# Moving the quantisation of the feed-forward weights from a stage of its own into the attention and layer-norm stages

## The chip, the cores and the metric

The kernel runs on the 8 cores of one Trainium2 chip. Each core computes one of the 8 sequences of the batch with all the weights; the cores exchange nothing. The metric is the device time in microseconds (us) of the slowest core; the time of a kernel is the median of its runs. The profile shows one execution, on its slowest core (core 1).

## The reference

One layer: attention with rotary embedding and a residual layer norm, then a feed-forward block whose weights are ternary and whose activations are 8 bit, then a second residual layer norm. Per core S = 2048 rows of D = 1024, 16 heads, inner width 4096.

```python
def _weight_quant(w):
    scale = 1.0 / jnp.clip(jnp.mean(jnp.abs(w)), 1e-05)
    wq = jnp.clip(jnp.round(w * scale), -1.0, 1.0) / scale
    return w + jax.lax.stop_gradient(wq - w)
def _act_quant(x):
    scale = 127.0 / jnp.clip(jnp.max(jnp.abs(x), axis=-1, keepdims=True), 1e-05)
    xq = jnp.clip(jnp.round(x * scale), -128.0, 127.0) / scale
    return x + jax.lax.stop_gradient(xq - x)
def _bitlinear(x, w):
    return jnp.einsum('bsi,oi->bso', _act_quant(x), _weight_quant(w))

x = _layernorm(x + attention(x, w_qkv, w_out))        # causal softmax, 16 heads
gate = jax.nn.silu(_bitlinear(x, w_gate))             # w_gate, w_up: 4096 x 1024
up = _bitlinear(x, w_up)
x = _layernorm(x + _bitlinear(gate * up, w_down))     # w_down: 1024 x 4096
```

`_weight_quant` needs the mean of |w| over a whole matrix of 4 M values before the first value of it can be quantised, so each weight is read twice. Rounding w/mean and clipping to -1, 0, 1 is the same as comparing w with plus and minus half the mean.

## The kernel before, in words

The program is written by hand: every engine has one list of instructions, run in order, and waits on counters (semaphores) that the other engines raise. `ve`, `se`, `te` count VectorE (DVE), ScalarE (ACT) and TensorE (PE) instructions, the counters that begin with `d` count DMAs (16 for each). DMAs are issued by SyncE (SP) or by GpSimd (POOL), in the order of that engine's list. The stages follow each other:

- **QKV and rotary.** Loads, projections, rotary on DVE.
- **Attention**, 64 pairs (head h, block j of 512 queries), with 4, 8, 12 and 16 key tiles for j = 0 to 3. For each pair PE makes the score tiles (L388, and L395 for the causal masks), ACT takes their exponential (L416), PE multiplies by V into one of two PSUM buffers `p_av` (L405). DVE copies the result out: for even heads straight into `s_aor` (L428), for odd heads into `s_odstb` (L435), from where POOL moves it by a DMA (L452), and the row sums into `s_dent` (L439), which POOL moves once a head (L457). PE starts the V product of pair i only after DVE's copies of pair i-2.
- **Normalisation.** Reciprocal of the row sums (L563 to L567) after the last of these DMAs, PE spreads it (L621), DVE scales `s_aor` (L634). POOL then loads `w_out` (L703).
- **Layer norm 1**, 16 tiles of 128 rows (`nt`). PE makes the output projection (L769); DVE adds the residual (L796) and sums (L800); ACT squares (L860), takes a square root (L862) and normalises (L867); DVE takes the largest |y| (L824), rounds to 8 bit (L835 to L845); PE transposes (L782), DVE copies (L851); SP stores both forms. Within a tile this is one chain from engine to engine, and DVE's list holds the tiles one after the other.
- **Weight quantisation**, pass A then pass B, over 48 tiles: 8 of 128x4096 for gate, 8 for up, 32 of 128x1024 for down, through two buffers `g_wst`. Pass A: SP loads (L932), ACT sums |w| (L941). Then three column sums (L969) and, per matrix, two tiny matmuls and two copies (L983, L993, L986, L995) give the thresholds `s_thr` on all partitions (L1002 to L1008). Pass B: SP loads again (L1022), DVE compares with the threshold above and below (L1036, L1039) and subtracts (L1043), POOL stores the result (L1052) in device memory. PE does nothing else meanwhile.
- **Feed-forward**, 4 groups of 512 rows: SP waits for all of the above and loads activations and ternary slices (L1386, L1396), POOL loads slices of the down matrix (L1456), PE runs L1528, L1542, L1502.

## Time and profile before

| | us |
|---|---|
| two runs | 2953.07, 2952.4; median 2952.73 |
| the profiled execution | 2948.69 |
| its span, first to last instruction, slowest core | 2947.1 |
| spans of the 8 cores | 2925.5 to 2947.1 |
| busy: PE, DVE, ACT, POOL | 1598.5, 1246.1, 636.3, 213.7 |

The time of the profiled execution is the span and 1.6 us around it. Busy shares are means over stages with different limits; the stages have to be read one at a time. In the rows below a row of a timeline gives start, duration, engine, line, operation, output and inputs, and in brackets how long the engine sat idle before it and what ended that. Rows that group instructions end with the number of them, their busy time, the mean of one in ns, and the idle time before them.

### The profile page before, as it was taken

What the parts mean: (1) busy time and instruction counts of PE and PEld (TensorE: products, weight loads), DVE (VectorE), ACT (ScalarE), POOL (GpSimd) and SP (SyncE); (2) the same over time, 40 slices, a digit from 0 to 9 for tenths busy, and PEclk for the clock granted to TensorE, in tenths of its full rate; (3) what the DMA queues carried; (4) which work ended last, traced back from release to release, by engine and by line L of the source; (5) the groups of instructions that cost most, each with busy time, mean ns of one, the idle gap of its engine ahead of it and who ended that gap; (6) DMA issues with size and microseconds to landing.
All of it is one profiled execution on the core that took longest, in us unless ns stands there. A gap on an engine that the chain in (4) does not pass through costs nothing.

```text
span 2947.1 us, 22422 instructions; the slowest of 8 cores (2925.5 to 2947.1 us)
## 1 busy us (share of the span) xinstructions
PE 1598.5 (54%) x6348; PEld 646.7 (22%) x6348; DVE 1246.1 (42%) x1935; ACT 636.3 (22%) x1082; POOL 213.7 (7%) x348
## 2 busy tenths in 40 slices
PE   0992069999996743400000005909864886397553
PEld 0441012333332211100000002404322332243221
DVE  0015621111113267740047663495646454744743
ACT  0310036666663011125410001101101110110010
POOL 1001200000000000000000110000020002001121
PEclk9996568888886576655555557959987899699887
DMA  9001200000000222249579775323522443152232
GB/s 170 9 1 36 57 22 6 5 5 5 5 4 5 44 72 79 85 159 319 184 251 315 266 225 176 116 72 100 154 79 68 129 139 96 51 143 81 69 115 100
DMA packets 135819, 295.90 MB, mean 100 GB/s; under 512 B 25987, under 2 KB 95878, under 8 KB 129286
## 3 DMA queue, kind: packets, MB, share of 16 engines
q1 hardware_dynamic: 108822, 204.01, 21.9%
q0 software_dynamic: 26880, 90.46, 11.0%
q8 instruction: 58, 0.95, 0.1%
q14 instruction: 59, 0.48, 0.1%
HBM read 250.13 MB, written 46.14 MB: 101 GB/s over the span
## 4 chain that ended last, share of the span: by engine, by line
PE 42%; DMA 20%; DVE 18%; issue 6%; ACT 5%; DVEq 5%; another core or an unknown queue 3%; POOL 1%; ACTq 0%; SPq 0%; POOLq 0%
DMA h_td<-ternd 7%; PE p6a L1528 7%; PE p6a L1542 7%; PE p_sc L388 6%; PE p_av L405 6%; PE p6a L1502 5%; PE p_qk L201 4%; PE p_sc L395 3%; DMA g_wst<-wdT 2%; ACT a_E L416 2%; DMA ternd<-g_tern 2%; PE p_qk L215 2%; PE p_R L621 2%; DMA g_wst<-wgT 2%
## 5 line engine op out<-in xcount | busy, mean ns | idle before, releaser
L1528 PE MATMUL p6a<-h_tg,h_xql 128*128 128x512 bf16 x1024 | 249.5, 388 | 342.4 <-DMA h_tu<-ternu 298.9
L416 ACT ACTIVATE a_E<-p_sc 128x512 bf16<-128x512 f32 x640 | 333.5, 627 | 195.5 <-PE p_sc L395 108.6
L1502 PE MATMUL p6a<-h_td,h_hqT 128*128 128x512 bf16 x1024 | 264.6, 407 | 153.9 <-DMA h_td<-ternd 140.7
L388 PE MATMUL p_sc<-a_q,a_k 64*128 64x512 bf16 x640 | 242.2, 418 | 180.6 <-DMA e_sel<-sel 151.7
L1542 PE MATMUL p6a<-h_tu,h_xql 128*128 128x512 bf16 x1024 | 244.3, 382 | 0.0
L1528 PEld LDWEIGHTS p6a<-h_tg,h_xql 128*128 128x128 bf16 x1024 | 101.5, 99 | 467.5 <-issue 351.6
L405 PE MATMUL p_av<-a_E,a_v 128*65 128x512 bf16 x640 | 187.1, 446 | 2.9 <-ACT a_E L416 2.9
L1275 DVE TENSOR_TENSOR h_h<-h_sg,p6a 128x512 f32<-128x512 bf16 x128 | 87.9, 687 | 226.8 <-PE p6a L1542 221.3
L1332 ACT ACTIVATE h_sg<-p6a,h_sc 128x512 bf16<-128x512 f32 x128 | 88.0, 687 | 427.7 <-PE p6a L1528 330.8
L1502 PEld LDWEIGHTS p6a<-h_td,h_hqT 128*128 128x128 bf16 x1024 | 98.4, 103 | 319.4 <-issue 239.0
L1456 POOL DMA_DIRECT2D h_td<-ternd x128 | 92.5, 723 | 919.2 <-PE p6a L1502 903.6
L201 PE MATMUL p_qk<-a_xfm,a_wqk 128*128 128x512 bf16 x512 | 112.1, 382 | 75.5 <-DMA a_wv<-wqkv 75.5
L388 PEld LDWEIGHTS p_sc<-a_q,a_k 64*128 64x128 bf16 x640 | 56.9, 95 | 353.7 <-issue 342.3
L1563 PE MATMUL p6t<-c_ident,h_hq 128*128 128x128 bf16 x512 | 50.4, 274 | 146.1 <-DVE h_hqT L1254 123.8
L1542 PEld LDWEIGHTS p6a<-h_tu,h_xql 128*128 128x128 bf16 x1024 | 101.1, 99 | 123.7 <-issue 5.0
L1338 ACT ACTIVATE h_sg<-h_os 128x512 bf16<-128x512 f32 x16 | 10.1, 630 | 525.4 <-DVE h_os L1219 525.4
L395 PE MATMUL p_sc<-a_masks,c_ident 128*128 128x512 bf16 x256 | 120.7, 472 | 0.0
L428 DVE CAST d_aor<-p_av 64x512 bf16<-64x512 f32 x32 | 21.8, 682 | 232.2 <-PE p_av L405 232.2
L435 DVE CAST a_odstb<-p_av 64x512 bf16<-64x512 f32 x32 | 21.8, 682 | 220.8 <-PE p_av L405 220.8
L249 DVE CAST a_v<-p_qk 128x512 bf16<-128x512 f32 x32 | 22.2, 694 | 219.1 <-PE p_qk L215 219.1
L983 PE MATMUL p_m<-c_consts,g_red 128*1 128x1 f32 x6 | 0.6, 163 | 208.8 <-DVE g_red L969 208.0
L941 ACT ACTIVATE g_trash<-g_wst 128x1024 bf16<-128x1024 f32 (+1 forms) x48 | 91.7, 1910 | 97.9 <-DMA g_wst<-wdT 53.4
(124 smaller groups left out, 1860.7 us busy)
## 6 DMA issues: line engine op xcount, KB each, us to landing
g_wst<-wgT SPq DMA_DIRECT2D x16, 2048.0 KB, 10.3
g_wst<-wuT SPq DMA_DIRECT2D x16, 2048.0 KB, 9.9
g_wst<-wdT SPq DMA_DIRECT2D x64, 512.0 KB, 4.3
h_td<-ternd POOLq DMA_DIRECT2D x128, 256.0 KB, 3.2
h_tg<-terng SPq DMA_DIRECT2D x32, 1024.0 KB, 8.4
h_tu<-ternu SPq DMA_DIRECT2D x32, 1024.0 KB, 11.0
f_xt<-x SPq DMA_DIRECT2D x16, 512.0 KB, 4.3
y1s<-f_y1n SPq DMA_DIRECT2D x16, 512.0 KB, 2.6
```

Source lines behind the costliest of these rows:

```text
L201: mm = t.matmul(pb[:], s_wqk[:, kc * 2048 + sl * 128: kc * 2048 + (sl + 1) * 128], s_xfm[:, kc * S + ntile * 512: kc * S + (ntile + 1) * 512],
L388: mm = t.matmul(pb[:], s_k[hp * 64: hp * 64 + 64, ch * S + kc * 128: ch * S + (kc + 1) * 128], s_q[hp * 64: hp * 64 + 64, ch * S + j * 512 ...
L395: mm = t.matmul(pb[:], s_ident[:], s_masks[:, r * 512:(r + 1) * 512], start=False, stop=True)
L405: mm = t.matmul(pv[:], s_v[:, vbase: vbase + 65], s_E[:, kc * 512:(kc + 1) * 512], start=(kc == 0), stop=(kc == nkc[(h, j)] - 1))
L416: se.inc(s.activation(s_E[:, kc * 512:(kc + 1) * 512], p_sc[kc % 4][:], AF.Exp, bias=-CSTAB, scale=0.125))
L941: se.inc(s.activation(s_trash[:, 0:wid], s_wst[i % 2][:, 0:wid], AF.Abs, accum_out=s_msum[:, i:i + 1]))
L1275: V(("hTT", j, gi), lambda v, j=j, gi=gi, o=o, k=k: v.tensor_tensor(s_h[k][:, o * 512:(o + 1) * 512], s_sg[gi % 2][:], p_a[1 if gi % 2 == ...
L1332: SEO(("silu", j, gi), lambda s, j=j, gi=gi, k=k: s.activation(s_sg[gi % 2][:], p_a[0 if gi % 2 == 0 else 2][:], AF.Silu, scale=sc2c(j, k, ...
L1456: dTd[dn % 2].dinc(g.dma_start(out=outap, in_=inap))
L1502: mm = t.matmul(p_a[k][:], s_hqT[k][:, kc * 128:(kc + 1) * 128], s_td[dn % 2][:, kk * 512:(kk + 1) * 512], start=(g2 == 0 and kk == 0), st ...
L1528: mm = t.matmul(pg[:], s_xql[j % 2][:, kc * 512 + k * 128:kc * 512 + (k + 1) * 128], s_tg[gs % 2][:, kc * 512:(kc + 1) * 512], start=(kc = ...
L1542: mm = t.matmul(pu[:], s_xql[j % 2][:, kc * 512 + k * 128:kc * 512 + (k + 1) * 128], s_tu[gs % 2][:, kc * 512:(kc + 1) * 512], start=(kc = ...
```

## The change

The stage of weight quantisation is taken out. Its work is cut into 96 chunks of 128x1024 (32 for each matrix) and put into the lists of two earlier stages; all its DMAs are now issued by POOL, through two buffers `t_wst`.

- **Pass A in the attention stage.** After POOL's work for pair i it issues loads up to chunk 1.5(i+1); load L waits until the sum of chunk L-2 is done. After its copies of pair i DVE sums |w| of the chunks up to 1.5(i+1) with `tensor_reduce`, each after its load.
- **Thresholds** at the head of layer norm 1: PE's six small matmuls come after its wait for `w_out` and ahead of the first output projection, DVE's copies and scalings ahead of its first tile.
- **Pass B in layer norm 1.** After tile `nt` ACT does two Sign activations for each of six chunks, sign(w - t) and sign(w + t), into the single buffers `s_ta` and `s_tb`; it begins chunk i only when DVE has added chunk i-1. After tile `nt` DVE adds the two for each of the six chunks. The sum is 0 or plus or minus 2, where it was 0 or plus or minus 1, so the scales of the feed-forward stage get 1/127 for 2/127. POOL: load chunk i, wait for the addition of chunk i-1, store it, load chunk i+1.
- SP and POOL wait for all counters of the earlier stages before the feed-forward stage.

```diff
         def _(v):
+            def _passA(v, hi):
+                while tern_emitA[0] < hi:
+                    i6 = tern_emitA[0]
+                    v.wait_ge(dW5[i6 % 2].h, pvW(i6))
+                    tpA.inc(v.tensor_reduce(s_msum[:, i6:i6 + 1],
+                                            s_wst[i6 % 2][:], AXX, ALU.add,
+                                            apply_absolute_value=True))
+                    tern_emitA[0] += 1
...
+                _passA(v, ((pi + 1) * NWCH) // len(pairs))
+            _passA(v, NWCH)
...
         def _(g):
+            def _loadA(g, hi):
+                while tern_emitL[0] < hi:
+                    L = tern_emitL[0]
+                    if L >= 2:
+                        g.wait_ge(tpA.h, L - 1)
+                    dW5[L % 2].dinc(g.dma_start(out=s_wst[L % 2][:],
+                                                in_=WCHUNKS[L][1]))
+                    tern_emitL[0] += 1
...
+                    slot += 1
+                    _loadA(g, (slot * NWCH) // len(pairs))
...
+            for i6 in range(NWCH):
+                L = NWCH + i6
+                if i6 < 2:
+                    g.wait_ge(tpA.h, NWCH)
+                else:
+                    g.wait_ge(ts2.h, 2 * (i6 - 2) + 2)
+                dW5[L % 2].dinc(g.dma_start(out=s_wst[L % 2][:],
+                                            in_=WCHUNKS[i6][1]))
+                if i6 >= 1:
+                    g.wait_ge(tv2.h, i6)
+                    dTst[(i6 - 1) % 2].dinc(g.dma_start(
+                        out=WCHUNKS[i6 - 1][2], in_=s_tn[(i6 - 1) % 2][:]))
...
             t.wait_ge(dWo.h, dG_wout)
             t.wait_ge(ve.h, ve_p3)
+            t.wait_ge(dS.h, dS_ones1)
+            for mi6 in range(3):
+                t.wait_ge(thrV.h, 3 if mi6 == 0 else 2 * mi6 + 2)
+                thrT.inc(t.matmul(p_m1[:], s_red[:, mi6:mi6 + 1], CC(1.0),
+                                  start=True, stop=True))
+                t.wait_ge(thrV.h, 2 * mi6 + 4)
+                thrT.inc(t.matmul(p_m2[:], s_ones1[:], s_t11[:],
+                                  start=True, stop=True))
...
+            def _combs(v, hi):
+                while tern_emitC[0] < hi:
+                    i6 = tern_emitC[0]
+                    v.wait_ge(ts2.h, 2 * i6 + 2)
+                    if i6 >= 2:
+                        v.wait_ge(dTst[i6 % 2].h, (i6 // 2) * 16)
+                    tv2.inc(v.tensor_tensor(s_tn[i6 % 2][:], s_ta[:], s_tb[:],
+                                            ALU.add))
+                    tern_emitC[0] += 1
...
+                _combs(v, ((nt + 1) * NWCH) // NT)
...
+            def _signs(s, hi):
+                while tern_emitS[0] < hi:
+                    i6 = tern_emitS[0]
+                    if i6 == 0:
+                        s.wait_ge(thrV.h, 12)
+                    s.wait_ge(dW5[i6 % 2].h, pvW(NWCH + i6))
+                    if i6 >= 1:
+                        s.wait_ge(tv2.h, i6)
+                    mi6 = WCHUNKS[i6][0]
+                    ts2.inc(s.activation(s_ta[:], s_wst[i6 % 2][:], AF.Sign,
+                                         bias=s_thr[:, 4 + mi6:5 + mi6],
+                                         scale=1.0))
+                    s.drain()
+                    ts2.inc(s.activation(s_tb[:], s_wst[i6 % 2][:], AF.Sign,
+                                         bias=s_thr[:, mi6:mi6 + 1],
+                                         scale=1.0))
+                    s.drain()
+                    tern_emitS[0] += 1
...
+                _signs(s, ((nt + 1) * NWCH) // NT)
...
-            for i, (mi, ti) in enumerate(tiles):
-                dsrc, ddst, ntl, wid = mats[mi]
-                s.wait_ge(dW5[dS5_evt[i][0]].h, dS5_evt[i][1])
-                se.inc(s.activation(s_trash[:, 0:wid], s_wst[i % 2][:, 0:wid],
-                                    AF.Abs, accum_out=s_msum[:, i:i + 1]))
-                s.drain()
...
-                ve.inc(v.tensor_scalar(s_ta[:, 0:wid], s_wst[i % 2][:, 0:wid],
-                                       CC(1.0), s_thr[:, mi:mi + 1],
-                                       ALU.mult, ALU.is_ge))
...
-                ve.inc(v.tensor_tensor(s_tern[i % 2][:, 0:wid], s_ta[:, 0:wid],
-                                       s_tb[:, 0:wid], ALU.subtract))
...
             sy.wait_ge(dTst[1].h, dO_p5[1])
+            for _h6, _v6 in tern_totals:
+                if _v6:
+                    sy.wait_ge(_h6, _v6)
```

## Rows read from the trace of the kernel before

**Rows 1.** Windows by stage: stretch, its length, busy us of each engine, PE clock, DMA share, GB/s.

```profile
394.00:937.00 543.00, 503.99 (x1536) 160.98 (x1536) 89.92 (x130) 334.74 (x641) 24.66 (x48) 0.83 0.02 5
1026.70:1293.40 266.70, 103.54 (x384) 43.65 (x384) 187.36 (x368) 42.76 (x65) 0.00 (x0) 0.65 0.24 74
1293.40:1499.80 206.40, 0.00 (x0) 0.00 (x0) 0.00 (x0) 97.38 (x97) 0.00 (x0) 0.50 0.72 245
1499.80:1777.60 277.80, 2.22 (x12) 1.82 (x12) 186.01 (x156) 0.00 (x0) 35.15 (x47) 0.50 0.81 271
```

**Rows 2.** Timeline at both ends of the quantisation stage.

```profile
1292.48 0.85 DVE L851 COPY f_xqst<-p_tr 128x512 bf16<-128x512 bf16 x2 [1.01 <-PE p_tr L782]
...
1776.84 0.69 DVE L1043 TENSOR_TENSOR g_tern<-g_ta,g_tb 128x1024 bf16<-128x1024 bf16 x1
...
1778.07 0.54 POOL L1052 DMA_DIRECT2D ternd<-g_tern  x1 [2.98 <-DVE h_sc L1261]
...
1780.56 1.30 SPq L1386 DMA_DIRECT2D h_xql<-xqs  x2
```

**Rows 3.** Timeline of DVE in attention: an odd head's last pair, then three of an even head.

```profile
466.95 0.68 DVE L435 CAST a_odstb<-p_av 64x512 bf16<-64x512 f32 x1 [12.40 <-PE p_av L405]
467.64 0.69 DVE L439 COPY a_dent<-p_av 1x512 f32<-1x512 f32 x1
470.65 0.68 DVE L428 CAST d_aor<-p_av 64x512 bf16<-64x512 f32 x1 [2.32 <-PE p_av L405]
...
484.47 0.68 DVE L428 CAST d_aor<-p_av 64x512 bf16<-64x512 f32 x1 [6.93 <-PE p_av L405]
```

**Rows 4.** Timeline at the end of attention.

```profile
931.18 0.69 DVE L439 COPY a_dent<-p_av 1x512 f32<-1x512 f32 x1
932.42 0.52 POOL L452 DMA_DIRECT2D d_aor<-a_odstb  x1 [13.72 <-DVE a_dent L439]
932.94 0.50 POOL L457 DMA_DIRECT2D d_denall<-a_dent  x1
934.76 1.33 DVE L563 TENSOR_SCALAR e_recip<-d_denall,c_consts 16x2048 f32<-16x2048 f32 x1 [2.90 <-DMA d_denall<-a_dent]
```

**Rows 5.** Groups of instructions by line and shape.

```profile
L824 DVE TENSOR_REDUCE f_st<-f_y1n 128x1 f32<-128x1024 f32 x16 | 19.5, 1220 | 23.7 <-ACT f_y1n L867 23.7
L860 ACT ACTIVATE f_tr<-f_y 128x1024 bf16<-128x1024 f32 x16 | 16.9, 1057 | 158.7 <-DVE f_y L796 158.7
L867 ACT ACTIVATE f_y1n<-f_y,f_st 128x1024 f32<-128x1024 f32 x16 | 19.8, 1240 | 12.4 <-DVE f_st L821 12.4
L1043 DVE TENSOR_TENSOR g_tern<-g_ta,g_tb 128x1024 bf16<-128x1024 bf16 x32 | 22.2, 692 | 3.3 <-issue 0.4
```

**Rows 6.** Timeline of the thresholds, first and last of their six round trips.

```profile
1500.69 0.19 PE L983 MATMUL p_m<-c_consts,g_red 128*1 128x1 f32 x2 [207.96 <-DVE g_red L969]
...
1505.03 0.16 DVE L995 COPY p_thr<-p_m 128x1 f32<-128x1 f32 x1 [0.80 <-PE p_m L986]
```

**Rows 7.** Landing of DMAs: x count, KB each, median us; last L1464, the POOL load h_y1t.

```profile
g_wst<-wdT SPq DMA_DIRECT2D x64, 512.0 KB, 4.3
h_y1t<-y1s POOLq DMA_DIRECT2D x16, 512.0 KB, 4.2
f_wout<-wout POOLq DMA_DIRECT2D x8, 256.0 KB, 11.4
...
DMA to landing us min/median/max: 3.5/4.2/5.3
```

**Rows 8.** Timeline inside layer norm 1: hand-overs between DVE and ACT.

```profile
1070.06 0.16 DVE L817 RECIPROCAL f_st<-f_st 128x1 f32<-128x1 f32 x1
1070.32 0.20 ACT L862 ACTIVATE f_st<-f_st 128x1 f32<-128x1 f32 x1 [2.24 <-DVE f_st L817]
1070.62 0.16 DVE L819 TENSOR_TENSOR f_st<-f_st 128x1 f32<-128x1 f32 x1 [0.40 <-ACT f_st L862]
```

**Rows 9.** Groups: ACT's table loads.

```profile
L1347 ACT ACT_TABLE_LOAD x3 | 3.8, 1283 | 1.0 <-DVE h_st L1238 1.0
L416 ACT ACT_TABLE_LOAD x1 | 1.3, 1283 | 207.5 <-PE p_sc L395 207.5
L941 ACT ACT_TABLE_LOAD x1 | 1.3, 1283 | 20.5 <-DMA g_wst<-wgT 20.5
```

More of the change, by code:

```diff
@@ L318, in build_program, with pvW, _ @@
         s_denall = mk(scD, "d_denall", [16, S], side="right")
+        s_wst = [mk(scD, f"t_wst{i}", [128, 1024], side="right")
+                 for i in range(2)]
+        s_msum = mk(scD, "t_msum", [128, 96], side="right")
+        s_red = mk(scD, "t_red", [128, 3], side="right")
+        s_t11 = mk(scD, "t_t11", [1, 1], side="right")
+        s_ones1 = mk(scD, "t_ones1", [1, 128], side="right")
+        s_ta = mk(scD, "t_ta", [128, 1024], BF16, side="right")
+        s_tb = mk(scD, "t_tb", [128, 1024], BF16, side="right")
+        s_tn = [mk(scD, f"t_tn{i}", [128, 1024], BF16, side="right")
+                for i in range(2)]
+        WCHUNKS = []
+        for mi6, (dsrc6, ddst6, ntl6, wid6) in enumerate(
+                ((d_wgT, d_terng, 8, 4096), (d_wuT, d_ternu, 8, 4096),
+                 (d_wdT, d_ternd, 32, 1024))):
+            for ti6 in range(ntl6):
+                for cc6 in range(wid6 // 1024):
+                    WCHUNKS.append((mi6,
+                                    dsrc6[ti6 * 128:(ti6 + 1) * 128,
+                                          cc6 * 1024:(cc6 + 1) * 1024],
+                                    ddst6[ti6 * 128:(ti6 + 1) * 128,
+                                          cc6 * 1024:(cc6 + 1) * 1024]))
+        NWCH = len(WCHUNKS)
+        def pvW(L):
+            return ((L // 2) + 1) * 16
+        @block.sync
+        def _(sy):
+            dS.dinc(sy.dma_start(out=s_ones1[:], in_=d_ones1))
+        dS_ones1 = dS.n
         p_sc = [psB.enter_context(nc.psum_tensor(f"p_sc{i}", [128, 512], F32))
@@ L787, in build_program @@
         assert te_tr_end == trun4 == te4_0 + 4 * NT
+        tern_emitC = [0]
         @block.vector
         def _(v):
+            v.wait_ge(tpA.h, NWCH)
+            for mi6 in range(3):
+                v.drain()
+                thrV.inc(v.tensor_reduce(s_red[:, mi6:mi6 + 1],
+                                         s_msum[:, mi6 * 32:(mi6 + 1) * 32],
+                                         AXX, ALU.add))
+            for mi6 in range(3):
+                v.wait_ge(thrT.h, 2 * mi6 + 1)
+                v.drain()
+                thrV.inc(v.tensor_copy(s_t11[:], p_m1[:]))
+                v.wait_ge(thrT.h, 2 * mi6 + 2)
+                thrV.inc(v.tensor_copy(s_thr[:, mi6:mi6 + 1], p_m2[:]))
+            v.drain()
+            thrV.inc(v.tensor_scalar(s_thr[:, 0:3], s_thr[:, 0:3],
+                                     CC(1.0 / NW), CC(1e-5), ALU.mult, ALU.max))
+            v.drain()
+            thrV.inc(v.tensor_scalar(s_thr[:, 0:3], s_thr[:, 0:3],
+                                     CC(0.5), CC(1.0), ALU.mult, ALU.mult))
+            v.drain()
+            thrV.inc(v.tensor_scalar(s_thr[:, 4:7], s_thr[:, 0:3],
+                                     CC(-1.0), CC(0.0), ALU.mult, ALU.add))
+            v.drain()
+            def _combs(v, hi):
[7 more added lines that the diff above has]
+                    tern_emitC[0] += 1
             for nt in range(NT):
@@ L893, in build_program @@
             return nc
-        scD.close()
-        scF.close()
-        psC.close()
-        scG = _scope()
-        s_wst = [mk(scG, f"g_wst{i}", [128, 4096]) for i in range(2)]
-        s_trash = mk(scG, "g_trash", [128, 4096], BF16)
-        s_msum = mk(scG, "g_msum", [128, 48])
-        s_red = mk(scG, "g_red", [128, 3])
-        s_ta = mk(scG, "g_ta", [128, 4096], BF16)
-        s_tb = mk(scG, "g_tb", [128, 4096], BF16)
-        s_tern = [mk(scG, f"g_tern{i}", [128, 4096], BF16) for i in range(2)]
@@ L973, in build_program @@
-        ve_red = ve.n
-        te5 = te.n
-        vruns = ve.n
-        @block.tensor
-        def _(t):
-            t.wait_ge(dS.h, dS_ones1)
-            for mi in range(3):
-                t.wait_ge(ve.h, ve_red if mi == 0 else vruns + 2 * mi)
-                te.inc(t.matmul(p_m1[:], s_red[:, mi:mi + 1], CC(1.0),
-                                start=True, stop=True))
-                t.wait_ge(ve.h, vruns + 2 * mi + 1)
-                te.inc(t.matmul(p_m2[:], s_ones1[:], s_t11[:],
-                                start=True, stop=True))
@@ L1011, in build_program @@
-        ve_thr = ve.n
-        dS5b_evt = {}
-        @block.sync
-        def _(sy):
-            sy.wait_ge(se.h, se_p5a)
-            for i, (mi, ti) in enumerate(tiles):
-                dsrc, ddst, ntl, wid = mats[mi]
-                if i >= 2:
-                    sy.wait_ge(ve.h, ve_thr + (i - 2) * 3 + 2)
-                dW5[i % 2].dinc(sy.dma_start(out=s_wst[i % 2][:, 0:wid],
-                                             in_=dsrc[ti * 128:(ti + 1) * 128, :]))
-                dS5b_evt[i] = (i % 2, dW5[i % 2].n)
@@ L1045, in build_program @@
-        ve_p5c = ve.n
-        @block.gpsimd
-        def _(g):
-            for i, (mi, ti) in enumerate(tiles):
-                dsrc, ddst, ntl, wid = mats[mi]
-                g.wait_ge(ve.h, ve_thr + i * 3 + 3)
-                dTst[i % 2].dinc(g.dma_start(out=ddst[ti * 128:(ti + 1) * 128, :],
-                                      in_=s_tern[i % 2][:, 0:wid]))
-        dO_p5 = (dTst[0].n, dTst[1].n)
-        if "terng" in dbg:
-            @block.sync
-            def _(sy):
-                sy.wait_ge(dTst[0].h, dO_p5[0])
-                sy.wait_ge(dTst[1].h, dO_p5[1])
-                dS.dinc(sy.dma_start(out=dbg["terng"], in_=d_terng))
@@ L1441, in _ @@
             g.wait_ge(dTst[1].h, dO_p5[1])
+            for _h6, _v6 in tern_totals:
+                if _v6:
+                    g.wait_ge(_h6, _v6)
             g.wait_ge(dY1n[0].h, dS_p4[0])
```

133 lines of the change are left out of this document (37 added, 96 removed).

## The prediction, made before the changed kernel ran

> **What bounds the kernel now.** I read the windows by stage first. In the attention stage PE is busy 504 of 543 us, DVE only 90 and the DMA engines 2% of the time. In layer norm 1 DVE is busy 187 of 267 us; no other engine comes near, the stage is one chain through DVE, ACT and PE. In the two windows of the weight stage PE does nothing, ACT is busy 97 of 206 us and DVE 186 of 278 us, and DMA carries 245 and 271 GB/s [rows 1]. Then I read the timeline at the ends of this stage. DVE's last copy of layer norm 1 ends at 1293.33, its last subtraction of the weight stage at 1777.53, POOL issues the last store 0.54 us later and SP the first load of the feed-forward stage at 1780.56 [rows 2]. Nothing overlaps with these 484.2 us (1777.53 - 1293.33), and this is what the change takes out. The question is what the same work costs where it is put.
>
> **Pass A, inside attention.** 96 sums of 128x1024. The row with this operation and shape takes 1.22 us [rows 5], so 117 us more for a DVE that idles 453 us. It is hidden if DVE's copies of pair i still end before PE starts the V product of pair i+2. For even heads POOL runs ahead and the loads lie ready. For odd heads POOL issues them only after the copies of the pair. The tightest place is the last pair of an odd head, which has two chunks, followed by the short first pairs of the next head. The copies end at 468.33 [rows 3]. POOL wakes 0.54 us later and first issues the DMA of `s_odstb` in 0.52 us [rows 2, 4], so the first load is issued at 469.4. I take 4.3 us to land: a 512 KB load of the same shape takes 4.2 from POOL and 4.3 from SP [rows 7]. It lands at 473.7, its sum ends at 475.0, the second chunk's at 476.3. The copies of the next pair, ready at 470.65, end at 477.7. The V product that needs them belongs to the pair whose copies start at 484.47 [rows 3], and its 12 matmuls start about 5 us before, at 479.4. So 1.7 us are left and the cost is 0. Without that cover (a landing over 6.0 us) each further us costs 1 us at seven places. A gain is excluded, since PE's list has no less to do.
>
> The last pair has no cover. Before, the reciprocal starts at 934.76, after the small DMA that POOL issues at 932.94 [rows 4]. Now POOL issues two loads at 932.94 and 933.5. They land at 937.2 and about 938.8 (the second shares the engines), the sums end at 938.6 and 940.1, and the reciprocal starts about 940.2: **+5.4 us** (bounds 4.5 and 7, for landings of 3.5 and 5.3 [rows 7]).
>
> **Thresholds.** The three column sums run while PE waits for `w_out`. The six round trips do not: PE's first output projection stands behind them. From the first small matmul to the last copy they took 1500.69 to 1505.19, and the last matmul ends before that copy: **+4.3 us** [rows 6]. DVE's scalings then run beside the first projection.
>
> **Pass B, inside layer norm 1.** DVE's list now holds six additions behind each tile, and the next tile's chain begins after them. The chain itself stays as it is, 266.7 us for 16 tiles [rows 1], so what counts is the length of a batch of six. Two quantities set it.
>
> S is one chunk from ACT to DVE and back: two Signs and an addition. Sign is not in the trace. Its bounds are 1.06 us (same output type, no per-partition operand) and 1.24 us (two such operands, 32-bit output) [rows 5]; Sign has one such operand, I take 1.15. An addition is 0.69 [rows 5], a hand-over in each direction 0.10 [rows 8], the drain between the Signs the same. S = 0.10 + 1.15 + 0.10 + 1.15 + 0.10 + 0.69 = 3.3 us (bounds 3.1 and 3.5).
>
> L is the time from the end of addition i until chunk i+2 has landed, since POOL issues that load behind the store of chunk i: 0.54 to wake, 0.54 for the store [rows 2], 4.3 for the load: 5.4 us. Bounds: a landing of 3.5 gives 4.6; one of 5.3 [rows 7] and 0.3 of slower issue give 6.7.
>
> ACT does the first chunk of a batch during the chain, so the first addition ends at 0.75. Chunk 1 has also landed, but its Signs wait for addition 0, because `s_ta` and `s_tb` are single. From there addition i+2 ends at the later of (addition i+1) + S and (addition i) + L + S. With L = 5.4 and S = 3.3 the second term wins at additions 2 and 4, so the additions end at 0.75, 4.05, 9.45, 12.75, 18.15 and 21.45. A batch is 0.75 + 2(L + S) + S = 21.45 us, and 16 make **+343 us**. With both low bounds it is 0.75 + 15.4 + 3.1 = 19.25, in all 308; with both high ones 0.75 + 20.4 + 3.5 = 24.65, in all 394. The stores (256 KB, 3 to 5 us) are awaited only two additions on. PE's projections have more time than before. SP's loads of x move up no queue, since the new DMAs are on POOL, and the stage drew 24% of the DMA engines [rows 1]; 75 MB more over about 600 us is 125 GB/s on top of 74, less than the 245 to 271 that the weight stage ran at with landings of 4.3 us.
>
> The trace gives the load 4.2 us [rows 7]. The Trainium skill (DMA: Bandwidth & Descriptors, "Anatomy of one DMA — SWDGE (gpsimd) path") has a DMA of GpSimd cost 2.0 us plus its bytes at 436 GB/s, 3.2 us here. By the page L would be 4.3, a batch 19.2 us, the stage 307 us longer, and the kernel 36 us faster than by the row; I go by the row, which has all eight cores loading.
>
> **Start of the feed-forward stage.** From the last addition to SP's first load the chain is the one of rows 2, 3.0 us, with 23 more waits on counters already reached. The trace shows none by itself. Bounds: 0, and 2.3 us at 0.10 each [rows 8]; I take +1.
>
> **Sum.** -484.2 + 5.4 + 4.3 + 343 + 1 = -130.5 us. Against the span of 2947.1 this gives 2816.6; against the profiled execution (2948.69) 2818; its time is 4.0 us under the median of the runs, 2952.73, against which I predict **2822 us**, 4.4% faster. With the low bounds of every term -484.2 + 4.5 + 4.3 + 308 = -167, 2785; with the high ones -484.2 + 7 + 4.3 + 394 + 2.3 = -77, 2876.
>
> **Rivals.**
>
> *Sign needs another function table than Sqrt.* Then ACT reloads twice a tile. The reload ahead of Sign hides in DVE's chain. The one on the way back stands ahead of Square or Sqrt, on the chain: 1.28 us [rows 9] times 16 is 21 us, so 2843. For it: ACT reloaded at L941 (Abs) although Square, Identity and Sqrt had just run [rows 9]. Against it: it also reloaded at L416, so it may do so at the start of every section of its list whatever the function. The Trainium skill (ScalarE: Activation LUTs, "Table sets: the hidden batching unit") says that cheap functions stand in every set as filler, Abs among them; then nothing is reloaded and the rival falls. The trace leaves that open: the load at L941 speaks against the page unless it is one per section. Chance 0.22.
>
> *Loads land late, and pass B runs at their pace.* This is the one that can end on the slower side. Everything else equal, the change stops paying where a batch takes (484.2 - 10.7)/16 = 29.6 us, that is L = 9.5, a landing of 8.4 us; it is 2% slower at a landing of 10.3. For it: POOL's loads of `w_out` took 11.4 us each [rows 7]. With that, L = 12.5, a batch 35.7 us, in all 571, plus 7 x 5.4 us of stalls in attention: -484.2 + 12 + 4 + 571 + 38 = +141, 3094 us. Against it: those were eight loads in flight at once, here there are at most two and a store. Chance 0.05 for slower, 0.06 for a landing in between that leaves it within 2%.
>
> *The load is hidden after all.* If it lands in under 2.2 us, or if POOL gets ahead in a way that I don't see, S alone sets the pace: a batch is 0.75 + 5 x 3.3 = 17.25 us, in all 276, and the kernel 2755 us. No load of 512 KB landed in under 3.5 us. Chance 0.05.
>
> *Attention is slowed* by DVE's late copies: only with a landing over 6 us, at 7 us for each us; it is in the high side of the forecast.
>
> **How the numbers follow.** The forecast, with the terms between their bounds, has 0.62; the table rival 0.22, late loads 0.11, hidden loads 0.05. 2% of 2952.73 is 59 us, about what a measurement of this kernel can tell from no change, so faster is below 2894. The forecast, the tables and the hidden load all end there, 0.89, less a little for a stall of another kind: 0.88. Within 2% 0.07, slower 0.05. The range goes from just under the lowest sum to the highest with part of the table loads: 2775 to 2880.
>
> **What would show it.** The profile after should have no stretch without PE work between layer norm 1 and the feed-forward stage; the attention stage as long as before; the reciprocal 5 us later; layer norm 1 at about 38.1 us a tile, of which 16.7 (266.7/16) as before, with DVE waiting alternately on ACT and on ACT that waited for a DMA of `t_wst`; Sign at 1.15 us; landings of 4.3 us. A tile of 39.4 us with table loads in it speaks for the first rival. Landings over 6 us, or PE waiting for DVE in attention, would make the forecast wrong upward; a batch under 19 us downward.

## The result

| | before | after |
|---|---|---|
| median of the runs, us | 2952.73 (2946.55 to 2987.42, 10 runs) | 2879.18 (2867.73 to 2900.02, 11 runs) |
| the profiled execution, us | 2948.69 | 2870.05 |
| its span, slowest core, us | 2947.1 (core 1) | 2868.4 (core 0) |
| busy PE, DVE, ACT, POOL, us | 1598.5, 1246.1, 636.3, 213.7 | 1581.2, 1242.8, 756.9, 333.1 |

The ratio of the times is 0.9722, with a 95% interval of 0.9675 to 0.9769: 2.8% faster, where 4.4% was forecast. The measured 2879 lies just inside the range, at its high end.

The windows by stage of the kernel after answer to [rows 1]: attention, layer norm 1 with pass B in it, the feed-forward stage. The columns are as there. The first window ends at the last copy of attention, while the one of [rows 1] also holds the normalisation's first steps up to 937.00, so their lengths can't be compared; the term for attention is in the table further down.

```profile
394.60:925.20 530.60, 489.05 (x1512) 159.49 (x1536) 201.55 (x222) 334.21 (x641) 73.53 (x138) 0.84 0.32 96
1031.90:1693.30 661.40, 103.72 (x376) 43.75 (x382) 252.54 (x466) 261.26 (x257) 101.00 (x189) 0.55 0.49 143
1693.30:2868.40 1175.10, 764.88 (x3520) 346.48 (x3584) 632.44 (x1153) 122.08 (x214) 102.03 (x145) 0.85 0.33 104
```

Layer norm 1 took 266.7 us by itself and takes 661.4 now. In it PE works 104 us, DVE 253 and ACT 261, and the DMA engines are busy half the time: no engine is full. It is a chain again, and the chain of what released what, for this stretch, says through what. Its summary by line, and then the pieces of the chain (start, duration, what) in one batch of six chunks:

```profile
by line: DMA t_wst<-wuT 10.5%; issue 9.7%; DMA t_wst<-wgT 9.3%; DMA t_wst<-wdT 8.7%; ACT t_tb L996 8.4%; ACT t_ta L992 8.3%; DVE t_tn L909 5.3%; DVE f_r L921 3.0%; ACT f_y1n L1010 3.0%; DVE f_xqtm L966 3.0%; DVE f_u L963 3.0%; DVE f_st L945
...
1262.08 0.69 DVE t_tn L909
...
1263.32 0.54 POOL terng L779
1263.86 6.43 DMA t_wst<-wuT
...
1277.56 0.54 POOL ternu L779
1278.10 6.39 DMA t_wst<-wuT
```

The landings of `t_wst` are 28.5% of this stretch. There are 32 such pieces on the chain, two in each of the 16 batches, as the recurrence of the prediction has them; together they are 188 us, 5.9 us each. The first of a batch takes 6.5 us in the mean, the second 5.3. The same batch in the timeline:

```profile
1262.08 0.68 DVE L909 TENSOR_TENSOR t_tn<-t_ta,t_tb 128x1024 bf16<-128x1024 bf16 x1
1262.24 0.37 SPq L808 DMA_DIRECT2D xqs<-f_xqst  x1
1262.70 0.53 SPq L812 DMA_DIRECT2D f_xt<-x  x1
1262.86 1.15 ACT L992 ACTIVATE t_ta<-t_wst,p_thr 128x1024 bf16<-128x1024 f32 x1 [7.71 <-DVE t_tn L909]
1263.32 0.55 POOL L779 DMA_DIRECT2D terng<-t_tn  x1 [15.72 <-DVE t_tn L909]
1263.86 0.53 POOL L775 DMA_DIRECT2D t_wst<-wuT  x1
1264.09 1.15 ACT L996 ACTIVATE t_tb<-t_wst,p_thr 128x1024 bf16<-128x1024 f32 x1
1265.40 0.69 DVE L909 TENSOR_TENSOR t_tn<-t_ta,t_tb 128x1024 bf16<-128x1024 bf16 x1 [2.64 <-ACT t_tb L996]
...
1270.43 1.15 ACT L992 ACTIVATE t_ta<-t_wst,p_thr 128x1024 bf16<-128x1024 f32 x1 [5.19 <-DMA t_wst<-wuT]
```

Both Signs, the addition and the hand-overs are as short as forecast: from the end of one addition (1262.77) to the end of the next (1266.09) it is 3.3 us. POOL wakes 0.55 us after the addition, issues the store of the chunk just done, and only then the load for a buffer that has been free for long (ACT's last Sign on it ended at 1255.15, its 7.71 us of idle time before 1262.86). ACT then waits 5.19 us for it. Three other transfers of this core start within 1.6 us of that load: the store of this chunk and SP's store and load for the tile. The landings of this stage (count, KB each, median us to landing), to be set against 4.3 in [rows 7]:

```profile
t_wst<-wuT POOLq DMA_DIRECT2D x32, 512.0 KB, 5.6
t_wst<-wdT POOLq DMA_DIRECT2D x32, 512.0 KB, 4.6
t_wst<-wgT POOLq DMA_DIRECT2D x30, 512.0 KB, 5.6
...
terng<-t_tn POOLq DMA_DIRECT2D x32, 256.0 KB, 3.7
...
ternd<-t_tn POOLq DMA_DIRECT2D x31, 256.0 KB, 2.4
```

The gate and up chunks, 128 pieces of 4 KB out of rows of 16 KB, take 1.0 us longer than the down chunks, which are one block of 512 KB.

The end of attention, which answers to [rows 4], and the thresholds, which answer to [rows 6]:

```profile
924.51 0.69 DVE L484 COPY a_dent<-p_av 1x512 f32<-1x512 f32 x1
925.78 0.54 POOL L511 DMA_DIRECT2D d_aor<-a_odstb  x1 [8.49 <-DVE a_dent L484]
926.30 1.08 POOL L500 DMA_DIRECT2D t_wst<-wdT  x2
927.38 0.50 POOL L518 DMA_DIRECT2D d_denall<-a_dent  x1
931.13 2.48 DVE L464 TENSOR_REDUCE t_msum<-t_wst 128x1 f32<-128x1024 f32 x2 [5.93 <-DMA t_wst<-wdT]
933.53 1.32 DVE L625 TENSOR_SCALAR e_recip<-d_denall,c_consts 16x2048 f32<-16x2048 f32 x1
```

```profile
1027.95 0.19 PE L843 MATMUL p_m1b<-c_consts,t_red 128*1 128x1 f32 x2 [20.92 <-DMA f_wout<-wout]
...
1031.88 1.06 PE L856 MATMUL p_o<-f_wout,d_aor 128*128 128x512 bf16 x2 [0.33 <-issue]
```

### The profile page after: what moved, and what is told of

Same layout as the page of the kernel before. It is cut to its first block, busy times and chain, and to the rows that moved or that the text cites. A ratio compares the mean times of both kernels' runs of the same rounds, so it can differ in the third digit from the quotient of the medians.

```text
span 2868.4 us, 23174 instructions; the slowest of 8 cores (2852.0 to 2868.4 us)
## 1 busy us (share of the span) xinstructions
PE 1581.2 (55%) x6237; PEld 646.5 (23%) x6348; DVE 1242.8 (43%) x1983; ACT 756.9 (26%) x1177; POOL 333.1 (12%) x588
## 4 chain that ended last, share of the span: by engine, by line
PE 42%; DVE 17%; DMA 17%; ACT 8%; issue 8%; DVEq 4%; another core or an unknown queue 3%; POOL 1%; ACTq 0%; SPq 0%; POOLq 0%
DMA h_td<-ternd 7%; PE p6a L1521 7%; PE p6a L1535 7%; PE p_av L440 6%; PE p6a L1495 5%; PE p_sc L423 5%; PE p_qk L206 4%; ACT a_E L451 3%; PE p_sc L430 3%; DMA t_wst<-wuT 2%; DMA t_wst<-wdT 2%; DMA t_wst<-wgT 2%; ACT t_tb L996 2%; ACT t_ta L992 2%
## 5 line engine op out<-in xcount | busy, mean ns | idle before, releaser
L856 PE MATMUL p_o<-f_wout,d_aor 128*128 128x512 bf16 x248 | 87.6, 527 | 344.7 <-DVE f_y L917 343.5
L464 DVE TENSOR_REDUCE t_msum<-t_wst 128x1 f32<-128x1024 f32 x96 | 116.2, 1219 | 227.1 <-DMA t_wst<-wdT 79.5
L909 DVE TENSOR_TENSOR t_tn<-t_ta,t_tb 128x1024 bf16<-128x1024 bf16 x96 | 66.3, 690 | 330.7 <-ACT t_tb L996 330.6
L992 ACT ACTIVATE t_ta<-t_wst,p_thr 128x1024 bf16<-128x1024 f32 x96 | 109.9, 1145 | 303.4 <-DVE t_tn L909 142.6
L856 PEld LDWEIGHTS p_o<-f_wout,d_aor 128*128 128x128 bf16 x256 | 31.5, 127 | 397.4 <-issue 388.7
L869 PE MATMUL p_tr<-c_ident,f_xqtm 128*128 128x128 bf16 x128 | 16.2, 306 | 190.2 <-DVE f_xqtm L966 190.2
```

Source lines behind the costliest of these rows:

```text
L464: tpA.inc(v.tensor_reduce(s_msum[:, i6:i6 + 1], s_wst[i6 % 2][:], AXX, ALU.add, apply_absolute_value=True))
L856: mm = t.matmul(pb[:], s_aor[:, kc * S + nt * 128:kc * S + (nt + 1) * 128], s_wout[:, kc * D + half * 512: kc * D + (half + 1) * 512], sta ...
L992: ts2.inc(s.activation(s_ta[:], s_wst[i6 % 2][:], AF.Sign, bias=s_thr[:, 4 + mi6:5 + mi6], scale=1.0))
```

## The experiments

"The stage" below is the time from the start of the first output projection to the start of the last addition or subtraction of pass B, the median over the 8 cores of a profiled execution. It is 748.8 us before (266.4 of layer norm 1 and 482.3 of weight stage) and 665.0 after. Rows of a view are from the slowest core of the run. In the cuts of the code `...` stands for lines left out, and remarks behind `#` are put in for the reader.

### Pass B in a stage of its own again

Pass A and the thresholds stay where the change put them; pass B goes back behind layer norm 1, as the kernel before had it.

```diff
-                _combs(v, ((nt + 1) * NWCH) // NT)      # DVE's list, after tile nt
-                _signs(s, ((nt + 1) * NWCH) // NT)      # ACT's list
-            for i6 in range(NWCH):                      # POOL's list: loads and stores
-                ...
+            for i, (mi, ti) in enumerate(tiles):        # SP, own stage
+                if i >= 2:
+                    sy.wait_ge(ve.h, ve_thr + (i - 2) * 3 + 2)
+                dW7[i % 2].dinc(sy.dma_start(out=s_wst[i % 2][:, 0:wid],
+                                             in_=dsrc[ti * 128:(ti + 1) * 128, :]))
```

> The changed kernel with pass B taken out of layer norm 1 again and put into a stage of its own behind it, as before the change (128x4096 tiles, SP loads, DVE compares); pass A stays in attention. Theory: pass A alone earns the gain and pass B inside layer norm 1 gives back more than its own stage cost (398 us longer against 278 us), so this kernel is faster than the changed one by 115 to 125 us: about 2755 us, ratio to before 0.933. Rival: moving pass B earned something too, since it fills idle engines; then this kernel is slower than the changed one, over 2880 us.

Measured: 2772.36 us (2759.07 to 2780.28), ratio to before 0.9344, interval 0.9264 to 0.9424. The windows of layer norm 1 and of the stage behind it:

```profile
1034.60:1302.40 267.80, 103.71 (x385) 43.54 (x385) 187.76 (x372) 42.76 (x65) 0.00 (x0) 0.65 0.23 74
1302.40:1592.40 290.00, 0.00 (x0) 0.00 (x0) 181.49 (x142) 0.00 (x0) 38.09 (x46) 0.50 0.77 258
```

The two together are 557.6 us, 107 less than the 665.0 of after, and the time fell by 107, a little under the 115 to 125 that were expected, since the stage of its own took 290 us and not 278. This is the finding of the study: **of the two moves only the first earns anything.** Pass A and the thresholds at their new places save 180 us (2952.7 - 2772.4); pass B in layer norm 1 costs 399 us where its own stage costs 278 [rows 1] to 290, and gives 107 to 121 of them back. In its own stage there are loads of up to 2 MB that run back to back at 258 GB/s; in layer norm 1 loads of 512 KB wait for additions that stand behind a tile's chain in DVE's list, while the buffers stand idle for the length of that chain.

### The load ahead of the store

POOL issues the load of chunk i+2 as soon as the Signs of chunk i are done, and stores chunk i behind it.

```diff
-                if i6 >= 1:
-                    g.wait_ge(tv2.h, i6)
-                    dTst[(i6 - 1) % 2].dinc(g.dma_start(
-                        out=WCHUNKS[i6 - 1][2], in_=s_tn[(i6 - 1) % 2][:]))
+                if i6 >= 2:
+                    g.wait_ge(tv2.h, i6 - 1)
+                    dTst[i6 % 2].dinc(g.dma_start(
+                        out=WCHUNKS[i6 - 2][2], in_=s_tn[i6 % 2][:]))
```

> Only POOL's order in pass B differs: load i+2 is issued as soon as the Signs of chunk i are done, ahead of the store of chunk i, not behind it. Theory that the load stands late because it is issued behind the addition and the store, and then shares the engines with that store: the load starts 1.4 us earlier (0.85 us for the addition, 0.55 us for the store) and lands in 4.5 us where it took 5.6; a batch is about 5 us shorter, layer norm 1 about 75 us shorter. Rival, that the 5.6 us come from all cores loading 16 KB strided rows at once and not from the store: the landing stays at 5.6 us, only the earlier start counts, 2.8 us a batch, 45 us in all.

Measured: 2813.54 us (2799.01 to 2817.94), ratio 0.949, interval 0.9421 to 0.9558; the stage 591.0, 74 less than after. The timeline inside a batch:

```profile
1284.13 0.69 DVE L910 TENSOR_TENSOR t_tn<-t_ta,t_tb 128x1024 bf16<-128x1024 bf16 x1 [2.64 <-ACT t_tb L997]
1284.51 0.53 POOL L775 DMA_DIRECT2D t_wst<-wuT  x1 [1.92 <-ACT t_tb L997]
...
1285.37 0.55 POOL L779 DMA_DIRECT2D ternu<-t_tn  x1 [0.34 <-issue]
...
1289.50 1.15 ACT L993 ACTIVATE t_ta<-t_wst,p_thr 128x1024 bf16<-128x1024 f32 x1 [2.21 <-DMA t_wst<-wuT]
```

The load is issued at 1284.51, 0.3 us before the addition ends, where it was issued 1.1 us after that end, and ACT waits 2.21 us for it instead of 5.19. The median landings of the gate and up loads fell to 5.0 us (from 5.6), and those of their stores rose to 5.0 and 5.1 (from 3.7): whichever of the two comes second takes longer. On the chain of waits the landings take 5.2 us in the mean, where they took 5.9. So 1.4 us of earlier issue and 0.7 of landing, twice in each of 16 batches, make 67 of the 74 us. The expected 75 us came out, but its 4.5 us for the landing did not: the gate and up loads still took 5.0.

### Chunks as whole rows

The 4096x1024 values of gate and up are cut as 32 contiguous blocks of 512 KB, as those of down are. Each value is handled alone, so any cut will do. Pass A in attention takes the same chunks.

```diff
-                                    dsrc6[ti6 * 128:(ti6 + 1) * 128,
-                                          cc6 * 1024:(cc6 + 1) * 1024],
+                                bass.AP(dsrc6.tensor, ti6 * 131072,
+                                        [[1024, 128], [1, 1024]]),
```

> Only the shape of the gate and up chunks differs: 32 whole rows of 4096, one contiguous block of 512 KB and a contiguous store of 256 KB, in place of 128 rows of 1024 at a pitch of 4096. Theory that the pitch makes these chunks land later than those of the down matrix (5.6 against 4.6 us in layer norm 1, stores 3.7 against 2.4): gate and up land in 4.6 us, a tile takes 39.5 us where it took 41.7, layer norm 1 is 20 to 25 us shorter. Rival, that the time of the gate and up tiles has to do with their place in the run and not with the layout: no change over 5 us.

Measured: 2854.02 us (2850.85 to 2878.22), ratio 0.9653, interval 0.9577 to 0.9728; the stage 642.2, 23 less than after, inside the 20 to 25 that were expected, though the landings did not come down to 4.6 us. The landings in layer norm 1:

```profile
t_wst<-wgT POOLq DMA_DIRECT2D x32, 512.0 KB, 5.1
t_wst<-wuT POOLq DMA_DIRECT2D x32, 512.0 KB, 4.9
...
terng<-t_tn POOLq DMA_DIRECT2D x32, 256.0 KB, 2.9
```

The landings on the chain are 5.22 us in the mean, 0.66 less than in after, and 32 of them make 21 of the 23 us. By time alone this kernel can't be told from after (the intervals overlap). The layout is one part of the longer landing, and not all of it.

### Two pairs of Sign buffers

Chunk i takes `s_ta[i % 2]` and `s_tb[i % 2]`, and its Signs wait for addition i-2, not i-1.

```diff
-                    if i6 >= 1:
-                        s.wait_ge(tv2.h, i6)
+                    if i6 >= 2:
+                        s.wait_ge(tv2.h, i6 - 1)
```

> Only s_ta and s_tb get a second buffer each, so the Signs of chunk i wait for the addition of chunk i-2 and not of chunk i-1. Theory that within a batch the loads set the pace and the single buffers cost only the step from the first to the second chunk, which has landed already: a batch is 2.5 to 3.5 us shorter, layer norm 1 about 45 us shorter. Rival, that the hand-over between ACT and DVE through the single buffers is the bound: each of five chunks saves 0.8 to 2.5 us, layer norm 1 is over 100 us shorter.

Measured: 2867.96 us (2864.06 to 2871.97), ratio 0.9682, interval 0.9617 to 0.9747; the stage 657.6, only 7 less. A miss. I had let the Signs of chunk i+1 run beside the load of chunk i+2 and shorten the batch by them. But the additions that set the batch are 0, 2 and 4: each waits for a load that is issued behind the addition two before, and then for the two Signs of its own chunk. The Signs of chunks 1 and 3 were already beside a load, and hiding them from DVE frees nothing. Only the last chunk of a batch gains, about 0.9 us, 14 us in all, and part of that went where the loads are now two at a time:

```profile
t_wst<-wuT POOLq DMA_DIRECT2D x32, 512.0 KB, 5.8
...
t_wst<-wgT POOLq DMA_DIRECT2D x30, 512.0 KB, 6.0
```

On the chain the landings are 6.10 us in the mean, 0.22 more than in after, and 32 of them are the 7 us that are missing.

### Load first and whole rows together

The two edits above in one kernel.

> The two changes to pass B's loads together: issued ahead of the store, and contiguous chunks. Alone they brought the gate landings in layer norm 1 from 5.6 us to 5.1 and to 5.0, and the stage from 665 us to 591 and to 642. Theory that store and layout are two causes that add: the gate and up chunks land in 4.5 us like the down chunks, and the stage takes 591 - 23, about 568 us. Rival, that a third cause (all cores drawing on the memory at once in this stage) holds them near 5: the second step brings under 10 us, 581 us or more.

Measured in two runs: 2795.78 us (2791.64 to 2799.93), ratio 0.9455, interval 0.9368 to 0.9543; the stage 578.0. The second edit brings 13 of the 23 us that it brought alone, less than the 23 of the theory and a little more than the 10 of its rival. The landings are 4.8, 4.7 and 4.5 us for gate, up and down, against 5.1, 4.9 and 4.5 with the second edit alone. On the chain they are 4.86 in the mean, 1.0 less than in after. So the two causes add only in part, and why gate and up stay 0.2 to 0.3 us above down with the same layout is open.

### Pass B spread through the chain

If the fault is that pass B stands behind the chain, it should be put into its gaps: six load buffers, three pairs of Sign buffers, three result buffers, contiguous chunks, the load ahead of the store. ACT does one chunk after the Square and five after the normalisation of a tile; DVE makes one addition at each of six places of a tile's chain, in front of instructions for which it would wait or drain anyway; five of them are of the same tile's chunks, and the first is the last chunk of the tile before.

```diff
+                _combs(v, 6 * nt)          # behind the sum of y
                 v.drain()
...
+                _combs(v, 6 * nt + 1)      # ahead of the wait for the normalised tile
                 v.wait_ge(se.h, se4_0 + nt * SE_PER + 3)
...
                 se.inc(s.activation(s_tr2[:], s_y1[:], AF.Square, accum_out=stc("sumsq")))
+                _signs(s, 6 * nt + 1)
...
-                _signs(s, ((nt + 1) * NWCH) // NT)
+                _signs(s, 6 * nt + 6)
```

> Pass B stays in layer norm 1 but is pipelined: six load buffers of its own with the next load issued after the Signs and ahead of the store, three buffers for the Signs and three for the result, contiguous chunks for all matrices, one chunk's Signs between Square and Sqrt and five behind the normalisation, and DVE's six additions spread between the steps of the tile's chain where it waits for ACT or PE. Theory that pass B cost 25 us a tile because it waited for itself, not because an engine was full: DVE then needs 16.3 + 6 x 0.69 less 2 us of filled waits, about 19 to 21 us a tile, layer norm 1 with pass B takes 310 to 340 us where it took 665, the kernel 2530 to 2560 us. Rival, DMA bandwidth: 5.9 MB a tile at the 245 to 270 GB/s of the old weight stage are 22 to 24 us a tile, 350 to 385 us, 2570 to 2600 us, with Signs waiting for loads in the trace.

Measured: 2519.59 us (2519.02 to 2522.18), ratio 0.8516, interval 0.8478 to 0.8554. It is 12.5% faster than after and 14.8% than before, and 10 us under the lowest time expected. The stage is 311.0 us, 19.4 a tile, where the chain alone takes 16.7. The window of the stage, and the landings in it:

```profile
1036.00:1340.00 304.00, 103.15 (x388) 43.85 (x388) 239.16 (x459) 249.70 (x249) 98.67 (x181) 0.63 0.92 305
```

```profile
t_wb<-wuT POOLq DMA_DIRECT2D x32, 512.0 KB, 6.5
t_wb<-wdT POOLq DMA_DIRECT2D x32, 512.0 KB, 6.5
```

The landings are longer than in any kernel above, and none of them stands on the chain of waits of this stretch, since up to six loads are under way. DVE's 239 busy us and ACT's 250 are nearly those of after (253 and 261) in less than half the time. The DMA engines are now 92% busy at 305 GB/s, so they are likely the next bound of this stage; no run tests that.

This kernel changes five things at once: the order of load and store, the layout, the number of load buffers, that of Sign and result buffers, and the place of the work. The first two together, in the experiment before, are 87 us of the 354 by which the stage is shorter than in after. The other 267 are not split between deeper buffers and places in the chain. An estimate from the rows: six additions of 0.69 us behind each tile's chain, with all loads and Signs hidden, would cost 4.1 us a tile, 66 in all, where the spread ones cost 45. So most of the gain may well be the depth of the buffers; no run tests it.

### The two ends

On top of the last kernel: pass A is dealt out over the first 62 pairs, so that the last pair has no chunk, and PE's six small matmuls stand ahead of its wait for `w_out`.

```diff
-                _passA(v, ((pi + 1) * NWCH) // len(pairs))
+                _passA(v, min(NWCH, ((pi + 1) * NWCH) // (len(pairs) - 2)))
...
-            t.wait_ge(dWo.h, dG_wout)
             t.wait_ge(ve.h, ve_p3)
...
+            t.wait_ge(dWo.h, dG_wout)
             for kind, nt in sched:
```

> As the interleaved kernel, with the two small costs at the ends taken away: pass A is spread over the first 62 pairs instead of 64, so that no chunk stands behind the last pair, and PE makes the threshold matmuls while w_out is still loading. Theory: the 4.8 us ahead of the reciprocal and the 4.0 us ahead of the first output projection both go, 8 to 9 us less than the interleaved kernel. Rival: the time from the last copy to the first projection is set by w_out's load and the wait moves there; then under 5 us less.

Measured: from the last copy of attention to the first output projection 98.1 us where it was 105.3 (medians of 8 cores), so 7.2 less, where 8 to 9 were expected. The reciprocal gives back its whole term, 5.0 us. The thresholds give back 2.3 of 4.0, and the rival is in part right. PE's projection now starts 0.1 us behind the last landing of `w_out`, where it started 4.0 behind it, and so the thresholds are hidden; but the eight loads of `w_out` took 20.0 us from the first issue to the last landing, where they took 18.5. They took 17.2 to 18.5 in before, after and the kernel with doubled sums too (medians), so the edit may have lengthened them; why is open. The time is 2525.07 us (2511.75 to 2539.66), ratio 0.852, interval 0.8455 to 0.8586: from the kernel without these edits it can't be told.

### Every sum made twice

Pass A in attention was forecast to cost nothing, and did. To see how far that cover reaches, DVE makes each sum of |w| a second time.

```diff
+                    v.tensor_reduce(s_msum[:, i6:i6 + 1],
+                                    s_wst[i6 % 2][:], AXX, ALU.add,
+                                    apply_absolute_value=True)
+                    v.drain()
                     tpA.inc(v.tensor_reduce(s_msum[:, i6:i6 + 1],
```

> The changed kernel with each of the 96 sums of pass A made twice (the same result written twice), 117 us more for DVE in attention. In an odd head DVE then needs about 4 x (1.4 copies + 1.1 wake and issue + 4.5 landing) + 6 x 2.44 = 42 us against the 33 us that PE needs for a head; the lateness is up to 9 us where the first pair of the next even head can bear about 8. Theory that pass A is free only while DVE's copies stay ahead of PE's second next V product: attention 5 to 25 us longer, with PE waiting for DVE's copies about every second head. Rival, that PE has enough to do in front of it and DVE is never late: attention unchanged within 2 us.

Measured in two runs: 2915.01 us (2909.27 to 2920.74), ratio 0.985, interval 0.9779 to 0.9921, 36 us over after. From the first score tile to the last copy, attention takes 565 us where it took 533 (medians of 8 cores): 33 us for 117 us more of DVE work. The waits of PE and of its weight loads in this kernel (us in total, times, longest), and then those of after:

```profile
PE p_av L440 <- DVE a_dent L488: 20.1, 8, 3.9
PEld p_av L440 <- issue: 92.5, 280, 4.2
```

```profile
PE p_av L440 <- ACT a_E L451: 2.9, 15, 0.2
PEld p_av L440 <- issue: 53.1, 200, 0.5
```

In after the V product waits for ACT alone, never for DVE, and no stall there is over 0.5 us. With twice the sums PE waits eight times for DVE's copy of the row sums, up to 3.9 us. This is the mechanism that the prediction names, a copy that comes too late for the product two pairs on. These waits are 8 to 23 us on the 8 cores, 18 in the median, inside the expected 5 to 25. They are not all of the 33. The window of attention in this kernel (core 3), and the one of after on a core with as many matmuls on record (core 1):

```profile
411.90:985.00 573.10, 518.50 (x1536) 165.76 (x1536) 314.30 (x316) 334.89 (x641) 73.53 (x138) 0.81 0.30 89
```

```profile
394.60:925.20 530.60, 495.36 (x1536) 159.34 (x1536) 201.66 (x222) 334.34 (x641) 74.15 (x140) 0.85 0.31 96
```

PE is busy 23 us longer with the same 1536 matmuls, at a granted clock of 0.81 where it was 0.85; over 8 cores it is 511 us instead of 495, 15 more. So about half of the loss is waiting for DVE, and the other half is PE's own work at a lower granted clock, which nothing in the expectation held. Why the clock fell is open.

## Why the prediction was off, step by step

| term, us | predicted | measured, medians of 8 cores |
|---|---|---|
| weight stage taken out | -484.2 | -482.3 |
| two chunks ahead of the reciprocal | +5.4 | +4.75 |
| thresholds ahead of the first projection | +4.3 | +4.0 |
| pass B in layer norm 1 | +343 | +398.7 |
| waits ahead of the feed-forward stage | +1 | +1.05 |
| attention | 0 | +0.5 |
| feed-forward stage | 0 | -1.2 |
| sum | -130.5 | -74.5 |

The profiled executions differ by 78.6 us and the medians by 73.6, so the table accounts for the change. One term carries the miss.

That the measured time lies inside the range is in part luck. It is 2879, over the 2876 that the sum gives with every term at its high bound; the range went on to 2880 only for a part of table loads that did not come. Pass B's term, 399 us, lies over its own high bound of 394, with a mean landing of 5.88 us over the 5.3 of that bound.

**Pass B's batch: the mechanism right, the landing too short.** The recurrence held: the chain of waits has exactly two landings in each batch. S was taken at 3.3 and is 3.33; Sign was taken at 1.15 and is 1.145 and 1.147:

```profile
L992 ACT ACTIVATE t_ta<-t_wst,p_thr 128x1024 bf16<-128x1024 f32 x96 | 109.9, 1145 | 303.4 <-DVE t_tn L909 142.6 <-DMA t_wst<-wuT 58.9 <-DMA t_wst<-wgT 52.0
L996 ACT ACTIVATE t_tb<-t_wst,p_thr 128x1024 bf16<-128x1024 f32 x96 | 110.1, 1147 | 8.1 <-issue 0.4
```

The wake and the store's issue were taken at 0.54 each and are 0.55 and 0.54. The landing was taken at 4.3 us and is 5.88 in the mean of the 32 that count. With that, L = 1.09 + 5.88 = 6.97, a batch 0.75 + 2(6.97 + 3.33) + 3.33 = 24.7 us, and sixteen 395; core 0 measured 395.5 (1694.04 - 1031.88 - 266.7). The step that failed is the sentence that takes 4.3 from [rows 7] because the rate stayed under that of the weight stage. The mean rate did stay under it, 143 GB/s against 271, and said nothing of one load: these loads start together with a store of the same chunk and two transfers of SP, and those of gate and up have another layout. The 4.3 was the median over down chunks alone. 32 landings longer by 1.58 us make 51 of the 56 us that the term missed. Contiguous chunks take 0.66 of the 1.58 away, the load ahead of the store 0.67, both together 1.0. The 0.6 us that are left, 19 us in all, have no cause shown. The first load of a batch starts beside SP's store and load, and it took 1.2 us more than the second in after; but with both edits it takes only 0.2 more (4.97 and 4.76) beside the same two transfers, and on two other cores of after the first and the second are alike (5.95 and 5.93, 5.78 and 5.92), so they are not the whole of that difference either.

The prediction set the rule of the Trainium skill (DMA: Bandwidth & Descriptors, "Anatomy of one DMA — SWDGE (gpsimd) path") beside its row: 2.0 us and the bytes at 436 GB/s, an estimate of 3.2 us for 512 KB. The landings of pass B did not come near it: the medians are 4.6 for a contiguous block and 5.6 for 4 KB pieces in layer norm 1, 6.5 with six loads under way. The measurement decides. The Trainium skill (DMA: Bandwidth & Descriptors, "Latency and other measured facts") adds that the fixed part of a DMA grows with the load on the device memory; the direction agrees with the 4.2 us in attention at 96 GB/s and the 6.5 at 305.

**What the prediction had in its own numbers and did not say.** It priced pass B at 343 us inside layer norm 1 and the same pass at 277.8 us in its own stage [rows 1], and never set the two beside each other. The move of pass B was a loss of 65 us by its own sum (121 as measured), paid for by pass A, whose 206 us went to nearly nothing. A change in two parts needs a sum for each part; the sum of both hid a better kernel, 107 us faster than the changed one.

**Attention at no cost: right.** The sum took 1.22 us as forecast, in a DVE that has the time:

```profile
L464 DVE TENSOR_REDUCE t_msum<-t_wst 128x1 f32<-128x1024 f32 x96 | 116.2, 1219 | 227.1 <-DMA t_wst<-wdT 79.5 <-DMA t_wst<-wuT 76.9 <-DMA t_wst<-wgT 69.6
```

The landings there were 4.5, 4.6 and 4.2 us for gate, up and down in the median, under the 6.0 up to which the prediction had cover. From the first score tile to the last copy the single cores took 529 to 538 us in both kernels, at granted clocks of 0.85 down to 0.83, so the +0.5 of the table is nothing. The doubled sums show that the cover is thin: with 1.2 us more for each chunk PE waits for DVE.

**The ends: right.** The reciprocal's predecessor starts 9.0 us after DVE's last copy (933.53 - 924.51), where it was 3.6 [rows 4]; over 8 cores the reciprocal is 4.75 us later. The thresholds hold PE from 1027.95 to 1031.88, 3.9 us.

**The table rival: fell.** In the whole of layer norm 1 ACT, which goes from Square to Sqrt to the normalisation and to Sign 16 times, loads its tables once, at the first Square of the section (a group by line):

```profile
L1003 ACT ACT_TABLE_LOAD x1 | 1.3, 1283 | 119.4 <-DVE f_y L917 119.4
```

So Sign asks for no other table than Sqrt, and the 21 us did not come. Whether the load at L941 in [rows 9] belonged to the start of a section or to Abs stays open: no kernel here has an Abs in another place, and the load above follows the exponentials of attention. The Trainium skill (ScalarE: Activation LUTs, "Table sets: the hidden batching unit") has cheap functions in every set, identity and abs among them; for Identity beside Sqrt the trace agrees, for Abs no run here shows it. The rival had a chance of 0.22, twice that of late loads, and it was the landing that deserved the doubt.

**Late loads, and loads hidden.** Both fell as named: the landing stayed below the 8.4 us of break-even and never came under 2.2. But the landings moved four tenths of the way to the first (1.58 of 4.1 us), between the bounds of the forecast and the rival, where the prediction had no chance set apart, and the bound of 5.3 from [rows 7] was too tight: it is the slowest of 16 loads of another stage. The predicted tile of 38.1 us was 41.3 on core 0.

## What to carry to other kernels

Price each part of a move both where it was and where it goes; a part that costs more at its new place should stay, whatever the sum over all parts says. Work that is to fill the gaps of a chain needs buffers deep enough that it never waits for itself, and places in the gaps: the same pass cost 399 us appended behind the chain's last instruction with two buffers, and 45 us (311.0 - 266.4) spread with six, contiguous and with the load first. Which of these brings how much was measured for the last two alone (87 us). Where a loop has a load on its chain, take the landing from a stage with the same layout, the same number in flight and the same neighbours on the queues, and issue the load for a free buffer before the store of a finished one.

## What the runs showed of the hardware

- The landing of one 512 KB load (median on the slowest core, all eight cores at work) ranged with its surroundings: 4.2 to 4.6 us in attention, and in layer norm 1 5.6 with 4 KB pieces behind a store, 5.0 with the same pieces ahead of the store, 5.1 and 4.9 contiguous behind it, 6.2 to 6.5 with up to six in flight. The last of these kernels is by far the fastest: a landing matters only where it is on the chain.
- Stores of 256 KB took 3.7 us in pieces and 2.4 to 2.9 contiguous, and 4.3 to 5.1 behind a load.
- A core moved 305 GB/s over 304 us with all eight cores at it, loads and stores of 256 and 512 KB from POOL and SP together, its DMA engines 92% busy.
- The granted clock of attention was 0.83 to 0.85 on the cores of after and 0.81 to 0.83 with every sum made twice, and PE's busy time for the same matmuls went with it (495 and 511 us in the median).
